# Second biases summed between the gate and the first gathered tile in expert layers 0 and 1; in the second graph layer norms one step later and three tiles' values projected inside its attention

## The reference

```python
    def _L1_gnn_ref(x, adj, W, a_src, a_dst):
        h = (x @ W.T).reshape(n, heads, out_dim)
        e_src = jnp.einsum('nhd,hd->nh', h, a_src)
        e_dst = jnp.einsum('nhd,hd->nh', h, a_dst)
        e = jax.nn.leaky_relu(e_src[:, None, :] + e_dst[None, :, :], negative_slope=0.2)
        ...
        alpha = jax.nn.softmax(e, axis=1)
        out = jnp.einsum('ijh,jhd->ihd', alpha, h).reshape(n, heads * out_dim)
    def _L1_ffn_ref(x, gate_w, gate_b, W1, b1, W2, b2):
        ...
        top2_vals, top2_idx = jax.lax.top_k(probs, 2)
        cw = jnp.zeros((N, Ee), dtype=xf.dtype).at[jnp.arange(N)[:, None], top2_idx].add(top2_vals)
        ...
            h = jax.nn.gelu(xf @ w1 + bb1, approximate=False)
            y = h @ w2 + bb2
            return (acc + we[:, None] * y, None)
```

## Time and profile before

| | |
|---|---|
| median of three runs | 1093.96 us (1091.34 to 1099.96) |
| profiled execution, its own time | 1096.7 us |
| its span | 1094.8 us |
| TensorE products, weight loads busy | 956.3 us (87%), 896.3 us (82%) |
| VectorE busy | 701.8 us (64%) |
| ScalarE, GpSimd busy | 514.7 us (47%), 445.4 us (41%) |
| mean granted TensorE clock | 0.926 of full speed |

### The profile page before, as it was taken

The page is one execution under the profiler, slowest core; times in us unless marked ns, Lnnn a source line. Parts: engine busy times, 40 slices in busy tenths (PEclk is TensorE's granted clock), DMA queues, the critical chain, the costliest instruction groups (busy, mean ns, idle before and its releaser), DMA issues. The chain is left out here.

```text
span 1094.8 us, 22761 instructions
## 1 busy us (share of the span) xinstructions
PE 956.3 (87%) x7554; PEld 896.3 (82%) x7554; DVE 701.8 (64%) x1653; ACT 514.7 (47%) x1001; POOL 445.4 (41%) x470
## 2 busy tenths in 40 slices
PE   6884999896899589989989899999889985999992
PEld 5584999786888579978979899999758875999992
DVE  3786777666899557776544466655656864666664
ACT  1252777134666357712045577767234532444341
POOL 1152577426776147621200145551244521344441
PEclk8797999798999789979989999999899995999997
DMA  7007865300000437322450011168200007655954
GB/s 250 2 25 241 312 219 178 97 1 1 11 10 11 183 109 269 135 83 95 129 195 8 16 35 38 38 220 308 92 2 5 11 21 268 255 168 172 322 162 135
DMA packets 57675, 132.30 MB, mean 121 GB/s; under 512 B 9664, under 2 KB 35712, under 8 KB 52864
## 3 DMA queue, kind: packets, MB, share of 16 engines
q1 hardware_dynamic: 47376, 106.45, 27.7%
q0 software_dynamic: 9024, 24.65, 7.4%
q10 hardware_dynamic: 1200, 0.23, 0.1%
HBM read 191.97 MB, written 17.56 MB: 191 GB/s over the span
## 5 line engine op out<-in xcount | busy, mean ns | idle before, releaser
L1959 PE MATMUL r_pH<-e_xsT,e_w 128*128 128x128 f32 x2304 | 281.5, 280 | 10.0 <-DVE e_xsT L2072 5.0
L1959 PEld LDWEIGHTS r_pH<-e_xsT,e_w 128*128 128x128 f32 x2304 | 272.4, 197 | 12.8 <-issue 9.6
L1914 POOL DMA_INDIRECT y_rows<-e_ys,e_to x94 | 156.8, 1668 | 190.6 <-DVE e_ys L2102 95.5
L1924 POOL DMA_INDIRECT e_xs<-xn_rows,e_idx x94 | 103.4, 1100 | 161.7 <-DVE e_idx L2076 120.4
L2088 DVE TENSOR_TENSOR e_w_lo<-e_w,e_w_hi 128x1024 fp32r<-128x1024 f32 (+1 forms) x74 | 113.4, 1532 | 13.8 <-ACT e_w_hi L2030 12.7
L1974 PE MATMUL r_pY<-e_w_hi,e_h_hi 128*128 128x256 f32 x384 | 114.5, 298 | 2.2 <-issue 2.2
L2030 ACT ACTIVATE e_w_hi<-e_w 128x1024 fp32r<-128x1024 f32 (+1 forms) x74 | 96.0, 1298 | 27.7 <-DMA e_w<-w_in 22.4
L498 ACT ACTIVATE g_t<-g_g,g_small 128x1024 f32<-128x1024 f32 x56 | 64.1, 1150 | 94.8 <-POOL g_small L485 94.8
L1974 PE MATMUL r_pY<-e_w_lo,e_h_hi 128*128 128x256 f32 x384 | 108.4, 282 | 0.0
L1974 PE MATMUL r_pY<-e_w_hi,e_h_lo 128*128 128x256 f32 x384 | 108.4, 282 | 0.0
L451 DVE SCALAR_TENSOR_TENSOR g_lm<-g_g,g_small,g_t 128x1024 f32<-128x1024 f32 x56 | 71.6, 1280 | 9.5 <-ACT g_t L498 7.0
(11 more groups left out here) (321 smaller groups left out, 1970.6 us busy)
## 6 DMA issues: line engine op xcount, KB each, us to landing
e_w<-w_in SPq DMA_DIRECT2D x56, 1024.0 KB
e_w<-w_in SPq DMA_DIRECT2D x84, 512.0 KB
e_w<-w_in SPq DMA_DIRECT2D x52, 514.0 KB
e_w<-w_in SPq DMA_DIRECT2D x24, 1028.0 KB
e_w<-y_rows SPq DMA_DIRECT2D x32, 256.0 KB, 5.4
p_adj<-adj_in SPq DMA_DIRECT2D x8, 512.0 KB, 11.3
xn_rows<-xn SPq DMA_DIRECT2D x32, 128.0 KB, 1.7
n_adjT<-adjT_in SPq DMA_DIRECT2D x8, 512.0 KB, 4.9
```

The costliest lines, as they stand in the source:

```text
L1914: pool.indirect_dma_start(out=y_rows[:, :], in_=ys[b][:, :], in_offset=None, out_offset=bass.IndirectOffsetOnAxis(ap=to[b][:, :], axis=0))\
L1924: pool.indirect_dma_start(out=xs[b][:, :], out_offset=None, in_=xn_rows[:, :], in_offset=bass.IndirectOffsetOnAxis(ap=idx[b][:, :], axis=0))\
L1959: ins = nc.tensor.matmul(pH[b % 2][:, f, :], w1[b][:, at:at + P], xsT[b % 2][:, c, :], start=(c == 0), stop=(c == DC - 1))
```

## The change

Three edits.

In layers 0 and 1 `GapBiases` takes the place of `SecondBiases`. The weights of the tokens (`vector_weights`) are worked out ahead of `vector_rows`; TensorE transposes `r_dense` behind the table's product and sums the biases in pairs of tiles, and VectorE adds four pairs behind `vector_dest`. The 56 unused products go. The load of b2 goes ahead of the experts' weights. At the end, TensorE waits for a signal behind the last tile (`tiles_over`) and goes on with the handover. Layer 2 keeps its order; in layer 3 only `vector_weights` moves ahead of `vector_rows`.

In the handover to the second graph layer, the values of tiles 5 to 7 (`EARLY = 5`) are neither multiplied nor kept. They are projected at the start of the attention's block, and ScalarE keeps them ahead of the first slope.

In that attention the norm, turn, logits and rank of each tile come one step later (`wait=2`), while GpSimd's rstd stays where it was.

```diff
                 ahead = 1
+                if "scalar_first" in extra:
+                    extra["scalar_first"](act)
                 slope_of(0)
...
         def attend(block, ph, front, heads, slope, lowest, rows, rest, values, width, finish, scores, done, free=0,
-                   settle=None, more=(), group=1, behind=4):
+                   settle=None, more=(), group=1, behind=4, wait=0):
...
             units = NT * heads
-            wait = behind - 4
+            power_at = min(wait, 1)
 
             def normed(t):
                 return done(t) + 1 + wait
...
             def pool_step(u, pool):
                 for t in range(NT):
-                    if done(t) + wait == u:
+                    if done(t) + power_at == u:
                         front.invert(pool, t)
...
-                          lambda u, c: V[:, c, u % H, :], DH + 1, finish, None, lambda t: (t + 1) * H + 4, group=H, behind=5)
+                          lambda u, c: V[:, c, u % H, :], DH + 1, finish, None, lambda t: (t + 1) * H + 4,
+                       more={"tensor": project, "scalar_first": place}, group=H, behind=5, wait=2)
```

```diff
                 if t >= 2:
                     pe.wait_ge(self.values_kept, t - 1)
-                for c in range(DC):
-                    nc.tensor.matmul(self.pv[t % 2][:, 0:D], xnT[:, c, q], self.w[:, c, :], start=(c == 0), stop=(c == DC - 1))
+                if t < self.EARLY:
+                    self.values(self.pv[t % 2][:, 0:D], t)
...
+            def values(self, pv, t):
+                for c in range(DC):
+                    ins = nc.tensor.matmul(pv, xnT[:, c, t * P:(t + 1) * P], self.w[:, c, :], start=(c == 0), stop=(c == DC - 1))
+                return ins
+
+            def keep_values(self, pv, t):
+                return nc.scalar.activation(self.V[:, t, :, 0:self.DH], pv.rearrange("p (h d) -> p h d", h=self.H), ACT.Copy)
...
                     act.wait_ge(self.valued, t + 1)
-                    nc.scalar.activation(self.rest[:, t, :], self.pv[t % 2][:, D:D + H], ACT.Copy, scale=1.0 - SLOPE)
-                    nc.scalar.activation(self.V[:, t, :, 0:DH], self.pv[t % 2][:, 0:D].rearrange("p (h d) -> p h d", h=H),
-                                         ACT.Copy).then_inc(self.values_kept, 1)
+                    ins = nc.scalar.activation(self.rest[:, t, :], self.pv[t % 2][:, D:D + H], ACT.Copy, scale=1.0 - SLOPE)
+                    if t < self.EARLY:
+                        ins = self.keep_values(self.pv[t % 2][:, 0:D], t)
+                    ins.then_inc(self.values_kept, 1)
...
+                spare = [ph.ps(f"front{n}", [P, 512]) for n in range(2)]
+                late, late_kept = ph.sem("late"), ph.sem("late_kept")
+
+                def project(pe):
+                    for t in range(before.EARLY, NT):
+                        if t >= before.EARLY + 2:
+                            pe.wait_ge(late_kept, t - before.EARLY - 1)
+                        before.values(spare[t % 2][:, 0:D], t).then_inc(late, 1)
+                    pe.wait_ge(late_kept, NT - before.EARLY)
+
+                def place(act):
+                    for t in range(before.EARLY, NT):
+                        act.wait_ge(late, t - before.EARLY + 1)
+                        before.keep_values(spare[t % 2][:, 0:D], t).then_inc(late_kept, 1)
```

```diff
+            def vector_weights(dve):
+                link = links[0]
                 dve.wait_ge(exped, 1)
...
-                    (vector_onehots, vector_slots, vector_tiles, vector_columns, vector_rows, vector_experts, vector_dest),
+                    (vector_onehots, vector_slots, vector_tiles, vector_columns, vector_weights, vector_rows, vector_experts,
+                     vector_dest),
...
+        class GapBiases:
...
+            def turn(self, pe):
+                pe.wait_ge(self.ready, 1)
+                for n in range(NT // DC):
+                    for part in range(DC):
+                        ins = nc.tensor.transpose(self.pT[n][0:self.E, part * P:(part + 1) * P], self.rows[:, n * DC + part, :],
+                                                  ident[:, :])
+                    ins.then_inc(self.turned, 1)
+
+            def keep(self, act):
+                for n in range(NT // DC):
+                    act.wait_ge(self.turned, n + 1)
+                    nc.scalar.activation(self.turned_rows[:, n * DC * P:(n + 1) * DC * P], self.pT[n][0:self.E, :], ACT.Copy)\
+                        .then_inc(self.kept, 1)
+
+            def sum(self, pe, rows_known):
+                pe.wait_ge(self.loaded, 16)
+                for pair in range(NT // 2):
+                    pe.wait_ge(self.kept, pair + 1 if pair < NT // 2 - 1 else NT // DC)
+                    if pair == 1:
+                        pe.wait_ge(rows_known, 1)
+                    if pair >= 2:
+                        pe.wait_ge(self.added, pair - 1)
+                    for t in (2 * pair, 2 * pair + 1):
+                        ins = nc.tensor.matmul(self.pS[pair % 2][:, t % 2, :], self.turned_rows[:, t * P:(t + 1) * P],
+                                               self.b2[:, :], start=True, stop=True)
+                    ins.then_inc(self.summed, 1)
+
+            def clear(self, pe, b):
+                pe.wait_ge(self.added, NT // 2 - 1 + b)
+
+            def add(self, dve, target):
+                for pair in range(NT // 2):
+                    dve.wait_ge(self.summed, pair + 1)
+                    two = slice(2 * pair, 2 * pair + 2)
+                    nc.vector.tensor_tensor(target[:, two, 0:D], target[:, two, 0:D], self.pS[pair % 2][:, :, :], ALU.add)\
+                        .then_inc(self.added, 1)
...
-                biases = SecondBiases(pr, E, b2_name, pT) if b2_name else None
+                gap = b2_name and not own_loaded
+                biases = GapBiases(pr, E, b2_name, pT, pY, pH) if gap else SecondBiases(pr, E, b2_name, pT) if b2_name else None
                 gate_tensor, gate_scalar, gate_vector, tiles_known, rows_known, turns_known = \
-                    gate(pr, L, E, all_probs, un, function, None if own_loaded else pY[1][:, 0:P], room, biases)
+                    gate(pr, L, E, all_probs, un, function, None if own_loaded or gap else pY[1][:, 0:P], room, biases)
...
+                    if gap:
+                        biases.load(sp)
```

```diff
                         pe.wait_ge(xsT_ready, t + 1)
                         if not early(i, b, 2):
                             pe.wait_ge(h_ready, t - 1)
+                        elif gap:
+                            biases.clear(pe, b)
...
                         ranks(pe)
                         table_of_pairs(pe)
+                        if gap:
+                            biases.turn(pe)
+                            biases.sum(pe, rows_known)
...
-                    if biases:
+                    if own:
                         biases.turn(pe, 3)
                         biases.sum(pe)
+                    if gap:
+                        pe.wait_ge(biases.tiles_over, 1)
                     after.tensor(pe)
...
                         slots(act)
                         column(act)
+                        if gap:
+                            biases.keep(act)
...
-                        for part in (slots, tiles, columns, rows, first_rows, experts_known, destinations):
+                        for part in (slots, tiles, columns, weights, rows, first_rows, experts_known, destinations):
                             part(dve)
+                        if biases:
+                            biases.add(dve, after.base)
...
                     end(last, UN - 1)
+                    if gap:
+                        nc.vector.memset(more[:, :], 0).then_inc(biases.tiles_over, 1)
                     after.vector_idle(dve)
-                    if biases:
+                    if own:
                         biases.add(dve, after.base)
```

More of the change, by code:

```diff
@@ L675, in pool_end @@
                 for t in range(NT):
-                    if done(t) + wait >= units:
+                    if done(t) + power_at >= units:
                         front.invert(pool, t)
@@ L685, in attend @@
                      "pool_step": pool_step, "pool_end": pool_end, "sync": sync}
-            for name in ("tensor", "scalar_early"):
+            for name in ("tensor", "scalar_early", "scalar_first"):
                 if name in more:
@@ L926, in build @@
         class BeforeGraph1(Handover):
-            H, DH, SLOPE = 4, 64, 0.2
+            H, DH, SLOPE, EARLY = 4, 64, 0.2, 5
             base = xn
@@ L1712, in add, with __init__, load @@
                                             self.pT[t % 2][:, :, :].rearrange("p c q -> p (c q)"), ALU.add).then_inc(self.added, 1)
+        class GapBiases:
+            def __init__(self, ph, E, name, pT, pY, pH):
+                self.E, self.name = E, name
+                self.pT = [t[:, :, :].rearrange("p c q -> p (c q)") for t in pT] + [t[:, :] for t in pY]
```

(16 more changed lines are left out.)

10 lines of the change are left out of this document (4 added, 6 removed).

## The result

The changed kernel takes 1107.8 us (median of 4 runs, 1106.5 to 1111.2) against 1093.9: a ratio of 1.0128, 95% interval 1.0099 to 1.0158. It is slower by 1.3%, and outside the range of 1082 to 1100. The profiled execution took 1107.0 us with a span of 1105.2, 10.4 us above the span before.

A forecast was written before the change was run, and what follows sets the result against it. VectorE was taken to bound the second graph layer, TensorE the expert loops and handover tail; +2.2 + 0.6 - 4.3 - 2.5 + 4.1 - 1.8 = -1.7 us gave 1092.3, range 1082 to 1100.

The forecast's parts named there:

- Bias products ahead of the first tile, +2.2: Layer 0's gate: transposes and bias products at clock 0.50 delay the first expert product from 107.85 to near 110.1, +2.2 us.
- Layer 1's gate, +0.6: Same bias chain behind layer 1's gate: first copy slips a little, gathers by up to 0.85, +0.6 us, bounds 0 and +1.5.
- Layer 0's end, -4.3: Layer 0's end: biases leave the path, stored rows' loads and beta's addition bound next, fewer transposes around last tile; -4.3 us.
- Values out of the tail, -2.5: Handover to second graph layer: TensorE's tail loses three tiles' values, which cost nothing in the attention; -2.5 us.
- Layer 1's end, -1.8: Layer 1's end: first sum 3.6 earlier, but TensorE's handover starts at a low clock; -1.8 us, ends 0 and -3.9.
- Norms one step later, +4.1: Second graph layer: each tile trades a 0.97 rstd wait for a 1.56 slope wait, +3.5, tail +0.6; +4.1 us.
- C: Second graph layer: a second slope late per tile through GpSimd's third instruction, 1.4 us each, 8.4; 1100.7 us, chance 0.08.
- A: Second graph layer: six rstd waits of 0.97 go and nothing comes back, -5.8 instead of +3.5; 1083.0 us, chance 0.20.
- B: Gates of both layers: the gap hides the biases, 2.8 less; 1089.5 us, chance 0.14.
- D: Ends of layers 0 and 1: loads' landing was the bound, first sums gain 1.0, layer 1 nothing; 1097.4 us, chance 0.06.
- E: Second graph layer: port rule as on the page, GpSimd gets in one instruction sooner, 0.25 per tile; 1090.8 us, chance 0.05.
- the three signs named for being wrong: Waits for slopes don't return in the second graph layer, the clock rises in the gates' gap, or stored rows land late.

The follow-up runs named there:

- rank_later: Changed kernel with only VectorE's rank in the second graph layer one step later still, behind the next mask and shift; 1098.4 us, ratio 1.0033.
- wait_kept: Changed kernel plus a VectorE wait for rstd at the step where the norm stood before, the norm itself staying a step later; 1098.3 us, ratio 1.0031.
- filled: Changed kernel with 16 unused TensorE products in each second-graph-layer tile, ahead of the products that the logits stand behind; 1102.4 us, ratio 1.0084.
- rank_later_wait_kept: Changed kernel with both edits, `rank_later` and `wait_kept`: rank one step later, VectorE's rstd wait at the norm's old step; 1095.2 us, ratio 1.0018.
- rouse_kept: Changed kernel with norm, turn, logits and rank back one step earlier, and the 56 unused products back behind layers 0 and 1's gate tables; 1088.3 us, ratio 0.9950.

## Why the prediction was wrong, point by point

- *Bias products ahead of the first tile, +2.2*: +2.7. The chain came as worked out (transposes 1.9, products 7.2 against 6.5, last addition 0.7), and that these products don't raise the clock was right: it stayed at 0.50.
- *Layer 1's gate, +0.6*: -0.2 by the marks of the table above, which is below its bounds of 0 and +1.5. From the end of the table's product, which the moved weights don't delay, to the first copy it took 10.12 us before and 10.37 after, so +0.25; 0.4 us of this are in the row above it.
- *Layer 0's end, -4.3*: -4.1, with the loads' landing as the next bound, as said.
- *Values out of the tail, -2.5*: -2.6.
- *Layer 1's end, -1.8*: -3.3 with its loop; the first sum came 3.6 us earlier and of it 1.0 was given back in the handover, where I had 2: TensorE stood idle for 6.21 us, and its first projection ran at a mean clock of 0.68.
- *Norms one step later, +4.1*: +22.5, and here is the step that failed. "With the norm a step later, each tile trades 0.97 for 1.56: +0.6" priced the late slope for VectorE alone. The price itself was met in the one trace that shows it alone: in `rank_later` the period is 13.83, 0.61 above before. What I left out is who else waits for that slope. In the tail I counted the rank's wait for logits that "now stand behind TensorE's last unit", and didn't ask the same of the other tiles. Before, the rank came in the second step behind a tile's end, and the logits ended at 309.94 where VectorE asked for them at 310.30, 0.36 us later. A step later they stand behind the products of a unit whose shift comes after the tile's end (1.9 us of small instructions), so that pause is no longer in their favour. In the sum the rank's wait in these tiles stood at nothing, without a reason; what the runs showed in its place is 1.59 to 3.65 us in each of five tiles.
- What the runs give for a tile, over the 13.2 before: 0.6 for the late slope alone (`rank_later`, 13.83); 1.2 for the rank's place with slopes on time (`wait_kept`, 14.45); 2.3 for both at the full clock (`filled`, 15.50); 3.9 to 4.3 with the clock at 0.50 in part of the tile (the changed kernel). The tail's longest wait is 7.8 instead of 3.6, though the whole stretch behind the sixth norm grew by 2.9 only.
- The rivals: C named a slope that comes late as the way to a slower kernel, and put 1.4 us per tile on it. Its sign was right for another reason: in the changed kernel L485 took 0.19 us behind the shift, and C's mechanism showed per tile only in `rank_later_wait_kept`. A is refuted, since a slope wait of 1.55 us came back in each tile. B failed in layer 0, where the clock stayed at 0.50 and the gate cost 2.7, and D, since the first sums gained 4.1 and 3.6 us. E would have changed 1.5 us; the rule of the Trainium skill's page "SBUF — State Buffer", section "Who interferes with whom", that the later instruction is blocked until the first has finished, would free L483 at 324.12 in the tile shown above, and it ended at 325.33, so here too the measurement is for two VectorE instructions, not one.
- The bounds of this term were -6 and +8.4, and both were bounds of GpSimd's lock; the wait of a third engine's consumer was outside of them. None of the three signs named for being wrong came (the slope waits returned, the clock didn't rise in the gap, the stored rows landed in time), so they couldn't have told of this loss.

## What to carry to other kernels

When an instruction is moved to a later step, compare for every consumer behind it the time at which it asks and the time at which its input came before. A slack of 0.36 us is a wait as soon as anything in its chain slips by more. A late input is to be followed through every queue that it holds (here ScalarE's exponential, TensorE's products, the logits, the rank), not only to the engine that waits for it first. And a short wait of the bounding engine can be what keeps the others in step.

## What was unexpected of the hardware

- Adding a wait of 0.97 us per tile on the bounding engine took 6.6 us off the stage (148.3 to 141.7), and 16 unused products per tile on TensorE took off 8.0.
- The late slope leaves TensorE idle for 2.05 us ahead of the products; twice the clock fell to 0.50 around the end of such a pause, and in and behind those stretches the wait for logits was 3.2 to 3.65 us instead of 1.59. With 1.16 us of it left (`filled`) four tiles of five kept 1.59.
- The granted clock stayed at 0.50 through 7.19 us of bias products (over 16 rows), and in `rouse_kept` it fell 1.25 us behind 3.96 us of them.
